# The 0/1 tables of the split portions, made in pieces of 128 edges between the low-row operations, in a graph layer on one core

## The reference

```python
msg  = xn[src] * edge_weight[:, None]
sums = segment_sum(msg, edge_type * N + dst)            # mean over each (relation, dst)
h    = sums / max(cnt, 1)
gnn  = einsum('rnc,rco->no', h, weight) + xn @ root + bias
x = x + gnn + linear_attention(xn)                      # 8 heads, elu + 1 features
x = x + experts(layernorm(x))                           # 6 experts of three layers, top 2 mixed
```

## Time and profile before

| | |
|---|---|
| median of 3 runs | 2996.17 us (2993.83 to 2996.44) |
| the profiled execution | 2996.88 us, its span 2995.4 us |
| granted TensorE clock, mean | 0.991 |
| TensorE busy | 2914.0 us, 97% of the span |
| VectorE busy | 2190.0 us, 73%, 5317 instructions |
| ScalarE busy | 1762.9 us, 59% |
| GpSimd busy | 1674.2 us, 56% |

### The profile page before, as it was taken

One profiled execution on the slowest core, in us unless ns is written; L12 is line 12 of the kernel. 1 busy time (PEld: TensorE's weight loads), 2 busy tenths in 40 slices (PEclk: granted clock), 3 DMA queues, 4 the chain that ended last, 5 costly groups with the idle time before them and its releaser, 6 DMA issues.

```text
span 2995.4 us, 47258 instructions
## 1 busy us (share of the span) xinstructions
PE 2914.0 (97%) x16707; PEld 2561.0 (85%) x16708; DVE 2190.0 (73%) x5317; ACT 1762.9 (59%) x3392; POOL 1674.2 (56%) x1700
## 2 busy tenths in 40 slices
PE   7999999979989999999999999999999999999998
PEld 5887878868878888888888988888988888888887
DVE  5489564145677887777788777778887777888775
ACT  4455555524456666665666666566665666666554
POOL 1000000052267777777777777777777777777750
PEclk9999999989999999999999999999999999999999
DMA  7777777765444434444443444444344444434430
GB/s 275 272 264 274 265 275 288 293 214 199 145 130 127 128 109 133 134 130 134 122 130 106 129 130 132 133 122 126 114 134 134 134 124 130 121 121 134 134 85 11
DMA packets 181936, 471.35 MB, mean 157 GB/s; under 512 B 46902, under 2 KB 105228, under 8 KB 159715
## 3 DMA queue, kind: packets, MB, share of 16 engines
q0 software_dynamic: 80544, 221.54, 25.6%
q1 hardware_dynamic: 98960, 244.93, 22.6%
q10 hardware_dynamic: 2196, 1.86, 0.2%
HBM read 310.71 MB, written 158.29 MB: 157 GB/s over the span
## 4 chain that ended last, share of the span: by engine, by line
PE 63%; POOL 6%; DVE 5%; issue 3%; ACT 1%; DVEq 1%; DMA 0%; SPq 0%; ACTq 0%; POOLq 0%
PE bank L1670 41%; PE acc L1727 7%; PE acc L1733 7%; POOL ring L1150 6%; PE acc L1670 2%; DVE sel L1381 2%; PE bank L1834 1%; PE bank L1697 1%; DVE x L1480 1%; PE bank L1706 1%; PE bank L1716 1%; DVE h_lo L1510 1%; DVE stats_c L1484 1%; PE bank L1783 1%; DVEq L1482 1%
## 5 line engine op out<-in xcount | busy, mean ns | idle before, releaser
L1150 POOL DMA_INDIRECT ring<-y_tab,tab x1666 | 1657.5, 995 | 633.8 <-issue 499.7
L1224 ACT ACTIVATE h_hi<-bank,bias_t 128x512 fp32r<-128x512 f32 (+1 forms) x600 | 407.3, 679 | 302.1 <-PE bank L1670 268.5
L1510 DVE TENSOR_TENSOR h_lo<-bank,h_hi 128x512 fp32r<-128x512 f32 (+1 forms) x600 | 382.0, 674 | 229.8 <-ACT bank L1225 227.8
L778 PE MATMUL yb<-wr_hi,xhl 128*128 128x512 f32 x1568 | 498.2, 394 | 13.1 <-ACT yst L355 11.1
L1210 ACT ACTIVATE row_hi<-ring,tab 128x256 fp32r<-128x256 f32 x1091 | 451.7, 498 | 33.3 <-issue 17.7
L1401 DVE SCALAR_TENSOR_TENSOR row_lo<-ring,tab,row_hi 128x256 fp32r<-128x256 f32 x1091 | 449.4, 478 | 9.4 <-ACT row_hi L1210 9.2
L1225 ACT ACTIVATE bank<-bank,bias_t 128x512 f32<-128x512 f32 (+1 forms) x600 | 386.3, 644 | 0.0
L355 ACT ACTIVATE yst<-yb 128x512 f32<-128x512 f32 x392 | 229.3, 596 | 249.4 <-PE yb L778 219.1
L778 PEld LDWEIGHTS yb<-wr_hi,xhl 128*128 128x128 f32 x1568 | 296.2, 189 | 79.9 <-ACT yst L355 15.8
L1670 PE MATMUL bank<-ew_hi,h_hi 128*128 128x256 f32 x1176 | 343.5, 292 | 1.6 <-DVE h_lo L1510 1.4
L1670 PE MATMUL bank<-ew_lo,h_hi 128*128 128x256 f32 x1176 | 330.8, 281 | 0.0
(11 more groups left out here) (265 smaller groups left out, 5506.6 us busy)
## 6 DMA issues: line engine op xcount, KB each, us to landing
y_tab<-yst SPq DMA_DIRECT2D x97, 1024.0 KB, 4.4
ring<-y_tab,tab POOLq DMA_INDIRECT x1666, 2.8
xt_tab<-xhl SPq DMA_DIRECT2D x25, 1024.0 KB, 4.8
xc<-xt_tab SPq DMA_DIRECT2D x25, 1024.0 KB, 5.5
xhl<-xt_tab SPq DMA_DIRECT2D x23, 1024.0 KB, 5.0
x<-x_tab SPq DMA_DIRECT2D x49, 256.0 KB, 3.1
xs<-in_x SPq DMA_DIRECT2D x24, 512.0 KB, 6.0
x_tab<-xs SPq DMA_DIRECT2D x24, 512.0 KB, 5.1
```

Of the source, the lines that this page charges most:

```text
L778: last = pe.matmul(out_ap, a, b, start=(i == 0), stop=(i == len(parts) - 1))
L1150: pool.indirect_dma_start(out=out_ap, out_offset=None, in_=y_tab[:, :], in_offset=bass.IndirectOffsetOnAxis(ap=idx_ap, axis=0)).then_inc(s ...
L1224: act.activation(dest[:, m, 0:W], b[:, 0:W], ACT.Relu, bias=bias)
L1510: gone(dve.tensor_tensor(lo_[:, m, 0:W], bank[plan[kind, (e, m)][0]][:, 0:W], hi[:, m, 0:W].bitcast(F32), ALU.subtract))
```

## The change

VectorE makes the table of a split portion in pieces, one for each block of 128 edges, each just ahead of that block's low rows, in place of one operation for the whole portion. In the loop the tables stood ahead of the expert's addition to `y`; now each piece stands where the low rows of its portion stand. `split` waits for the free buffers and for the high rows and then alternates. The code of portions 4 to 7 before the loop stays.

```diff
+                def split(n, p):
+                    if p >= parts(n):
+                        return
+                    tables_free(dve, n, p)
+                    dve.wait_ge(hi_ready, split_before(n, p) + 1)
+                    for q, (t, k) in enumerate(tiles_of_portion(p)):
+                        dve.tensor_tensor(hot_r[:, p % BUFS, q:q + 1, :], ramp[:, 0:NT].unsqueeze(1).to_broadcast([P, 1, NT]),
+                                          rel_w[:, n % 2, t, k:k + 1].unsqueeze(2).to_broadcast([P, 1, NT]), ALU.is_equal)
+                        last = dve.scalar_tensor_tensor(out=row_lo[:, p % SLOTS, q, :], in0=ring[:, p % SLOTS, q, :],
+                                                        scalar=tab[:, n % 2, t, k, 2:3],
+                                                        in1=row_hi[:, p % BUFS, q, :].bitcast(F32),
+                                                        op0=ALU.mult, op1=ALU.subtract)
+                    last.then_inc(lo_ready, 1)
+
                 def prepare(n, p):
                     if p < PLAIN:
                         weighted(n, p)
                     else:
-                        one_hot(n, p)
-                        low_rows(n, p)
+                        split(n, p)
...
-                        for p in coming:
-                            one_hot(i + 1, p)
                         if e == EXPERTS - 1 and i + 2 < SUPER:
...
                             if h == 0 and coming:
-                                low_rows(i + 1, coming[0])
+                                split(i + 1, coming[0])
...
                         for p in coming[1:]:
-                            low_rows(i + 1, p)
+                            split(i + 1, p)
```

## The result

The kernel with the change takes **3069.72 us** (median of 4 executions, 3065.06 to 3070.61), the kernel before 2995.0 in the same series (4 executions, 2991.61 to 2996.44): ratio 1.0248, 95% interval 1.0230 to 1.0266. It is 2.5% slower; the forecast of 3055 was 14.7 us short, inside its range. The profiled execution took 3070.61 us, with a span of 3069.1.

What follows compares the result with a forecast made beforehand. TensorE, busy 97% of the span, was taken as the bound. Stalls of 2.56 us in 23 iterations (58.9), plus 0.6 and 1.0, less 1.3, gave 59.2 us more: 3055 us against the median, range 3014 to 3100.

Steps and rivals of the forecast that it cites:

- The price of a pair: VectorE's time for one piece plus its low row: 0.60 us, using a spacing of 0.21 from the earlier trace.
- The first rival: No stall: pieces fill gaps between low rows, pair 0.435 us, kernel 2995 us; chance of no or nearly no stall 0.14.
- the third: Rival: pieces do not overlap at all, pair 0.77 us, kernel 3204 us; chance of dearer than 0.655 is 0.08.
- A: Hand-over of portion 6, in expert 1: VectorE finishes late and TensorE stalls 1.64 us an iteration.
- C: Hand-over of portion 10, in expert 3: TensorE stalls 0.67 us an iteration.
- D: Behind portion 10, four `rel_w` operations and two low parts end late for TensorE: 0.25 us an iteration.
- B: Hand-over of portion 8, in expert 2: -0.03 us, so no stall and no margin.
- E: Hand-over of portion 11, in expert 4: five pairs, no stall, covered by 0.91 us of idle time.
- The start: Four split portions made ahead of the loop with TensorE waiting: 0.3 to 0.37 us each, counted as 1.0 us.
- The 0.6 of the 24th pass: Last iteration, whose next group has only portion 5: `h1` of expert 3 waits 0.6 us for a bank.
- What may come back: Time lost to long GpSimd gathers inside low rows, at most 1.3 us over the loop, counted as gained.
- The second rival: Gathers were the true bound; pieces give GpSimd its turn: 2995 us; chance of no or nearly no stall 0.14.

Runs made afterwards that it cites:

- the place alone: The change with each portion's table whole in one operation, but at the new place behind the waits; 3031.72 us, ratio 1.0123 to the kernel before.
- pieces of two blocks: The change with pieces of two blocks (256 edges) in place of one, three for a portion of six; 3042.72 us in one execution.

## Why the prediction was right in kind and 15 us short

- **The price of a pair** was right: 0.593 us measured, 0.60 forecast, and with it the choice of the 0.21 of the earlier trace rows between the ends. The first rival (0.435) and the third (0.77) fall. The 0.258 us for a piece, an estimate from the cycles that the Trainium skill gives (VectorE: DVE Perf Modes, section on the TRN2 errata), is between the two numbers that the rows show: the next operation starts 0.20 us after the piece, which itself lasts 0.282. For the length of a row of operations the 0.20 counts.
- **The hand-overs** came where they were forecast and with their sizes: A 1.61 for 1.64, C 0.65 for 0.67, D 0.21 for 0.25; B, forecast without a stall or a margin, 0.05. E has no stall. The idle time that replaces the tables ahead of `y` (1.81 us), and ScalarE's release of the first piece, are as described.
- **The step that failed** is the sum "A + C + D = 2.56 us an iteration": it counts the waits and nothing for starting again. The runs showed 0.10 at each of five stops, 0.51 an iteration, 11.7 us in 23. That TensorE "pays more than the wait itself to start again" was named as a way to be wrong, with no price. The rows of before held a hint of it: the earlier trace rows shows the first matmul behind a wait with 0.58 us, where one inside a run has 0.28. Of the 14.7 us that the forecast is short these starts are 11.7, and the 1.3 that did not come back (below) are next; smaller stops take 0.9 off. The other 2.6 are less than executions of one kernel differ by (5.5 among the four).
- **The start** (1.0) is confirmed by the runs with the same start code. The 0.6 of the 24th pass came too: read from starts, `h1` of expert 3 is 0.69 late there, and 0.11 more for its start. It can't be seen in the length of the stretch behind the last row of the chain, which is 0.7 shorter after the change: later in that pass the clock was down for longer in the kernel before (granted 0.57 from 2954.0 to 2966.0 us) than in the kernel after (0.86 in the same part of the pass, 3028.4 to 3040.4).
- **What may come back** (1.3) did not: the kernel after has longer iterations of its own (up to 91.05), and its loop is 1.6 over 23 undisturbed ones, before 1.3.
- **A slip in the sums beside the forecast:** E is called covered by 0.91 us of idle time, yet the 3099 (at 0.654), the 3096 (at 0.65) and the upper end 3100 (at 0.655) count its 0.11 to 0.14 an iteration. Without it each is some 3 us less; the forecast of 3055 is not touched.
- Put together, the profiled execution of the change without its fall of the clock and without the 2.95 us ahead of the first `kv_bd` product is 2996.88 + 68.9 + 1.0 = 3066.8, inside the 3065.06 to 3070.61 measured.
- **The second rival** has its mechanism and not its effect. The long gathers go, 20 to none, shown by the change against the place alone. The gather of 2.39 us in the place alone agrees with the lock that the Trainium skill describes (SBUF — State Buffer, section "SBUF: two separate sides"), in which a VectorE operation with two SBUF inputs and a GpSimd one that reads SBUF keep each other out. The trace agrees only in part: 276 of the 296 gathers that start inside such low rows there took 1.23 us or less. What makes a gather one of the 20 was not tried. But GpSimd spends what it gains on waiting for TensorE (120 us).

## What to carry to other kernels

Work that stands ahead of a wait is free up to the length of the wait; moved behind it, it is paid as far as it goes beyond the consumer's margin, so before moving an operation ask at each hand-over how much margin the consumer leaves. Sum margins and prices by hand-over, and add a price for every new stop: here TensorE paid 0.10 us more than the wait, five times an iteration. Read a stop from the starts of the matmuls ahead of it and behind it, since the idle time in the bracket is counted from a modelled end and was short by 0.16 us at 256 columns.

## What the runs showed of the hardware

- Behind a stop TensorE's second matmul follows 0.22 us after the first instead of 0.12 at 256 columns, 0.34 instead of 0.23 at 512, even where the stop itself was only 0.05 us.
- A gather that GpSimd issues inside an unbroken row of low rows (two SBUF tensors each) can last until after the row's end: 2.39 us instead of the 0.95 that is the median. Few do: 20 of 310 in the kernel before, 20 of 296 with the place alone. An operation with one PSUM and one SBUF tensor ahead of every low row or every second one was enough to end it: none over 2 us among 414 gathers (the change) and 386 (pieces of two blocks).
- The granted clock fell for a part of five microseconds behind a stand of 2.39 us in one execution and not in two others with the same stand.
